# Narrow diagonal key blocks of query chunks 1 to 3 spread among the wide ones

## What is computed

```
x  = L0_attn_x                                    # 4 x 2048 x 256
xn = layernorm(x)
q, k, v = low-rank projections of xn              # rotary embedding on half of q and k
scores = (q @ k.T) / sqrt(16)                     # per batch and head, 2048 x 2048, causal
att = softmax(scores)
out = x + (att @ v) @ Wc + ffn(xn)
```

## Time and profile before

| what | value |
|---|---|
| median of 3 runs | 2284.16 us (2282.98 to 2284.55) |
| the profiled execution: its own time | 2280.11 us |
| the profiled execution: its span | 2278.3 us |
| attention: first to last product | 660.7 to 2150.2 us of the span |
| distance of one turn from the next (same instruction) | 92.75 us |
| mean granted TensorE clock | 0.943 of full |

### The profile page before, as it was taken

One profiled execution on the slowest core, in us unless ns is written; L12 is line 12 of the kernel. 1 busy time (PEld: TensorE's weight loads), 2 busy tenths in 40 slices (PEclk: granted clock), 3 DMA queues, 4 the chain that ended last, 5 costly groups with the idle time before them and its releaser, 6 DMA issues. The chain is left out here.

```text
span 2278.3 us, 50411 instructions
## 1 busy us (share of the span) xinstructions
PE 2095.3 (92%) x14033; PEld 799.9 (35%) x14033; DVE 1858.6 (82%) x4721; ACT 1560.9 (69%) x2068; POOL 338.1 (15%) x617
## 2 busy tenths in 40 slices
PE   6899999999799999999998999999999899999698
PEld 5455455455322222222222222222222222222155
DVE  5677877877789889798897988989889898899177
ACT  1655665665248778788787878878788788888600
POOL 1111111111210211102111121111211112111100
PEclk8999999999769999899998999989999999999879
DMA  3122232234330321303203032030330303300176
GB/s 148 56 76 76 83 87 61 84 86 92 93 51 2 49 36 15 50 2 48 41 10 50 2 48 41 9 50 2 48 48 2 50 2 49 48 2 12 35 225 206
DMA packets 146114, 123.95 MB, mean 54 GB/s; under 512 B 81984, under 2 KB 132500, under 8 KB 144404
## 3 DMA queue, kind: packets, MB, share of 16 engines
q1 hardware_dynamic: 137156, 112.46, 23.5%
q10 hardware_dynamic: 8720, 8.65, 1.3%
HBM read 69.50 MB, written 50.86 MB: 53 GB/s over the span
## 5 line engine op out<-in xcount | busy, mean ns | idle before, releaser
L1142 ACT ACTIVATE prob<-st 128x1024 f32<-128x1024 f32 (+3 forms) x1280 | 1080.0, 900 | 207.4 <-PE st L1265 194.3
L1241 PE MATMUL sm<-K,Q 48*128 48x512 f16 (+3 forms) x2304 | 650.8, 368 | 56.4 <-DVE pm L1204 19.4
L1204 DVE TENSOR_REDUCE pm<-sm 128x1 f32<-128x512 f32 x1024 | 648.7, 683 | 39.7 <-PE sm L1241 37.2
L1278 PE MATMUL pv<-prob,V 128*32 128x512 f32 (+3 forms) x5120 | 622.8, 562 | 0.1
L1189 DVE CUSTOM_DVE_ANT_0 sm<-sm,mask 128x128 f32<-128x128 f32 (+3 forms) x1024 | 490.6, 509 | 69.4 <-PE sm L1241 58.1
L1265 PE MATMUL st<-Q,K 50*128 50x512 f16 (+3 forms) x2560 | 496.6, 362 | 17.3 <-ACT prob L1142 14.7
L1241 PEld LDWEIGHTS sm<-K,Q 48*128 48x128 f16 x2304 | 174.3, 94 | 783.3 <-DVE pm L1189 326.8
L1094 POOL TENSOR_SCALAR_AFFINE_SELECT prob<-prob 128x256 f32<-128x256 f32 x512 | 205.7, 406 | 1284.1 <-ACT prob L1142 1279.5
L1200 DVE CUSTOM_DVE_ANT_0 sm<-sm,excess 128x512 f32<-128x512 f32 x256 | 172.9, 717 | 43.8 <-PE sm L1241 34.3
L1265 PEld LDWEIGHTS st<-Q,K 50*128 50x128 f16 x2560 | 135.0, 95 | 132.6 <-ACT prob L1142 84.9
L1278 PEld LDWEIGHTS pv<-prob,V 128*32 128x32 f32 x5120 | 104.4, 110 | 161.5 <-issue 130.3
(11 more groups left out here) (138 smaller groups left out, 1824.5 us busy)
## 6 DMA issues: line engine op xcount, KB each, us to landing
Q<-scratch_q SPq DMA_DIRECT2D x102, 128.0 KB, 4.3
K<-scratch_k SPq DMA_DIRECT2D x102, 128.0 KB, 6.5
x<-in_x SPq DMA_DIRECT2D x18, 512.0 KB, 4.6
scratch_v<-Vs SPq DMA_DIRECT2D x64, 128.0 KB, 2.0
scratch_r<-R SPq DMA_DIRECT2D x16, 512.0 KB, 3.2
V_raw<-scratch_v SPq DMA_DIRECT2D x16, 512.0 KB, 8.9
scratch_y<-Y SPq DMA_DIRECT2D x64, 128.0 KB
Yt<-scratch_y SPq DMA_DIRECT2D x16, 512.0 KB, 5.8
```

The lines of the kernel that those rows point to most:

```text
L1142: act.activation(prob[(slot * UNITS + u) % PT][:, :, 0:width], st[number % ST][:, :, 0:width], ACT.Exp)\
L1204: dve.tensor_reduce(out=pm[:, row, t, k:k + 1], in_=x, axis=AX.X, op=ALU.max).then_inc(sm_read, 1)
L1241: pe.matmul(dst[:, 0:block_width(t, k)], lhsT=Q[slot][r, h // 2, t * P:(t + 1) * P], rhs=K[slot][r, h // 2, k * CH:k * CH + block_width(t, ...
L1278: i = pe.matmul(pv[2 * DH * h:2 * DH * (h + 1), CH - width:CH], lhsT=V[slot][:, j, h, :], rhs=prob[(slot * UNITS + 2 * n + h // 2) % PT][: ...
```

## The change

The blocks of a chunk are listed by a function. Chunk 0 keeps its order. In chunks 1 to 3 the narrow blocks are set at even distances among the wide ones: chunk 1 reads 0, **5**, 1, 2, **6**, 3, 4, **7**; chunk 2 reads 0, 1, **9**, 2, 3, 4, **10**, 5, 6, 7, **11**, 8; chunk 3 reads 0, 1, 2, **13**, 3 to 6, **14**, 7 to 10, **15**, 11, 12 (narrow ones in bold). The flag that closes the accumulation and the planner's copy-out now go by the place in the list. No instruction is added or removed in the body of a turn, apart from register settings.

```diff
-ORDER = [(c, j, CH - P * max(0, j - SUB * c)) for c in range(TC) for j in range(SUB * (c + 1))]
+def key_blocks(c):
+
+
+    wide, narrow = list(range(SUB * c + 1)), list(range(SUB * c + 1, SUB * (c + 1)))
+    if c == 0:
+        return wide + narrow
+    step = len(wide) / len(narrow)
+    blocks = []
+    for n, j in enumerate(wide):
+        blocks.append(j)
+        blocks += [x for k, x in enumerate(narrow) if n < step * (k + 0.5) <= n + 1]
+    return blocks
+
+
+ORDER = [(c, j, CH - P * max(0, j - SUB * c)) for c in range(TC) for j in key_blocks(c)]
+LAST_BLOCK = [n + 1 == PAIRS or ORDER[n + 1][0] != ORDER[n][0] for n in range(PAIRS)]
...
-                if j == SUB * (c + 1) - 1:
+                if LAST_BLOCK[n]:
                     act = max(act, end + SIGNAL) + EVACUATION
...
-                                  start=j == 0, stop=j == SUB * (c + 1) - 1, tile_position=(0, 2 * DH * h))
+                                  start=j == 0, stop=LAST_BLOCK[n], tile_position=(0, 2 * DH * h))
```

## The result

| | before | changed |
|---|---|---|
| median of 4 runs | 2284.36 us | 2314.92 us |
| range | 2282.98 to 2285.65 | 2314.64 to 2316.02 |
| profiled execution, its span | 2278.3 us | 2312.7 us |
| attention, first to last copy of `pv` | 1481.1 us | 1513.6 us |
| an ordinary turn | 92.6 to 92.9 us | 94.2 to 94.5, or 95.8 to 96.2 us |

The ratio is 1.0138, 95% interval 1.0123 to 1.0153. The forecast was 2294 us, with a range up to 2312. The sign was right and the size was 31 us instead of 10. Attention holds 32.5 of the 34.4 us by which the two spans differ. The third kind of turn, the first behind each turn of the hardware loop, takes 96.5 to 97.8 us before and 98.5 to 100.3 us now.

What follows compares the result with a forecast made beforehand. TensorE was taken to pace the narrow stretches, TensorE with VectorE the wide ones. 15 turns x (1.0 - 0.4) + 1.0 for the last = +10.0 us gave 2294 us, range 2262 to 2312.

Steps and rivals of the forecast that it cites:

- Step (b): End of a turn: TensorE waits for the last wide block's mask, 0.75 to 1.25 us, booked as 1.0 us per turn.
- Step (c): End of a turn on VectorE: idle time grows from 0.56 to some 2 us, not added to Step (b).
- Step (a): Wide stretches of chunks 1 to 3: less TensorE waiting for ScalarE, 0.4 us off a turn, bounds 0 and 2.78 us.
- the term for the clock: TensorE's low clock: nothing booked in the forecast's sum; more low time appeared only as Rival 3.
- Rival 3: Turn's start: the stop lengthens TensorE's low clock, up to 1.7 us a turn, 2320 us; chance 0.08.
- Steps (d) and (e): GpSimd's `negate` and `place_v` stay hidden despite moved masks; SP's queue moves with entries and last product; nothing booked.
- Rival 1: VectorE paces: spreading closes its gaps in the narrow stretches, 1.97 us a turn, 2271 us, or 2258; chance 0.34.

Runs made afterwards that it cites:

- e3: Changed kernel, all three chunks spread, but with narrow block 15 as the last of chunk 3; ratio 1.0047 to the kernel before.
- e7: Changed kernel with a turn's last two entries moved from ahead of unit 78's scores to ahead of the last two products; ratio 1.0138 to the kernel before.
- e6: Blocks in the rising order of the kernel before, entries and excess units at the places planned for the spread order; ratio 1.0135 to the kernel before.
- e9: Against the kernel before, only chunk 3 spread, with block 15 last; ratio 0.9977.
- e8: Against the kernel before, chunks 2 and 3 spread, with block 15 last, chunk 1 in rising order; ratio 0.9996.
- e2: Against the kernel before, only chunks 1 and 2 spread, chunk 3 in rising order; ratio 1.0049.
- e12: e3 with chunk 1's last two blocks swapped, so a wide block closes it, entries planned anew; ratio 1.0010 to the kernel before.
- e4: Spread block order of the changed kernel, entries and excess units at the places planned for the rising order; ratio 1.0188 to the kernel before.
- e1: Changed kernel with only chunk 3 spread, chunks 1 and 2 in rising order; ratio 1.0056 to the kernel before.
- e10: Kernel before, in rising order, but with wide diagonal block 12 put last in chunk 3; ratio 1.0061.

## Why the prediction was wrong

**Step (b), the stop at the turn's end: right.** Said: 0.75 to 1.25 us on TensorE, ended by GpSimd's mask, 1.0 us taken, in every turn. Measured: 0.98 us, 16 times, 15.4 us. Its price by e3 is 1.15 us of chunk 3 per turn, 18 us in all against the 16 booked.

**Step (c): right in kind, too small.** VectorE's gap is 3.44 us, over the 2 to 3 us that were to show it. That it must not be added holds by e7.

**Step (a), the gain in the wide stretches: this step failed, by its sign.** With it failed the term for the clock, which the sum had at nothing (below). Step (a) said that the waits for ScalarE would shrink, that VectorE's gaps would not be touched directly by the widths, and took 0.4 us off a turn. At equal clock, turn 8 is 94.20 us against 92.61 before, or 92.65 in turns like it: +1.57 us, of which 1.15 is the turn's end, so the rest is **+0.42 us where -0.4 was booked**, 12 us over 15 turns. The waits point to why. Those for exponentials fell by 1.6 us over all of attention, a tenth of a microsecond a turn. Those of entries for a bank rose by 20.3 us, 1.3 a turn, since the planner put the entries at other places and TensorE's list is strict: an entry that is listed before VectorE has freed its bank holds up the main work behind it. That these waits are the loss is argued and not shown, since they and the time don't move in step (below), but e6 shows that new places for the entries can cost 1.35% by themselves. (Part of the 1.3 is regained: TensorE's busy time in that turn, a union of matmuls that overlap, is 87.75 against 88.27 us.) The lower bound of the step was zero gain, with no loss admitted, though the widths decide where the planner puts every entry. I read TensorE's full narrow stretches as work merely moved; they were also the stretches in which it hardly ever waited: 5.20 of 5.20, 5.09 of 5.10 and 6.19 of 6.26 us busy.

**Which chunk's spreading lost it.** Turns with equal low clock tell it: chunks 1 to 3 without any (mean of the three places of a turn in the loop), and a chunk 0 with 3.4 us of it. Before, that is 77.34 + 14.55 = 91.89 us. With chunk 3 spread (e9) it is 77.11 + 14.63 = 91.74, with chunk 2 as well (e8) 77.61 + 14.63 = 92.24, with chunk 1 as well (e3) 78.06 + 14.18 = 92.24, and with chunks 1 and 2 alone (e2) 78.32 + 14.18 = 92.50. So spreading chunk 3 did gain some 0.2 us a turn (0.15 by e9 against before, 0.26 by e3 against e2), spreading chunk 2 cost 0.5, and spreading chunk 1 cost next to nothing but the low clock at its seam, which e8 and e9 don't have. The waits for banks in e9, e8 and e3 are 32.2, 47.4 and 54.7 us: they rise with the 0.5 us of chunk 2, and again with chunk 1, where the time doesn't.

**Rival 3, the clock: the right kind at the wrong place.** It put another low spell behind the turn's start. There nothing grew: 15.1 to 15.2 us from one turn's last copy to the next, against 15.40 to 15.56 before. The new spells stand 36 us behind it, at the seam of chunks 1 and 2, in 7 turns: 7 x 1.58 = 11 us. I had named chunk 0 as the one sparse spell and did not look at what stands at a seam; turn 14 of the kernel before showed a fall at one. Its price, 1.58 us for 3.4 us of low clock, is near the 1.7 that I had.

**Steps (d) and (e): right.** Among the waits of the changed kernel's TensorE none is for `NK` or `V`, and none of its own for Q's transfers.

**Rival 1, VectorE paces: no.** No turn got shorter, and VectorE's idle time per turn rose from 92.61 - 83.03 = 9.6 to 94.20 - 82.66 = 11.5 us. But its opposite was too simple as well: VectorE is not the bound, and yet TensorE's waits for it grew by 20 us. By the Trainium skill's rule that I had weighed ("Trainium Kernel Development and Optimization", Performance Expectations), weight loads at 35% leave TensorE room. The runs show no such room at the turn's end, where the stop of 0.98 us went with 1.15 us of time (e3), and VectorE's gap was not the one to count: e7 cut its first part to 1.45 us and the time stayed as it was.

**The sum, with what was measured.** 15 turns x 1.57 = 23.6 us, low clock at the seam 11.1, the last turn 86.08 - 84.70 = 1.4: 36.1 us. Against it stand about 1 us in turn 11, whose low clock at the start was 3.4 instead of 6.8 us, 1.3 us for the low clock in turn 14 of the kernel before, and some 1.5 us in the four turns behind a loop's: 32.3, where attention shows 32.5. Of the 10 us forecast, (b) gave 16 and came to 18; (a) gave -6 and came to +6; the clock gave nothing and came to +11, less what was short elsewhere. (a) alone would have made 2306, inside the range; (a) and the clock together left it.

**Left open.** By medians the way from the changed kernel to e3 is 0.9%, to e12 another 0.37%, to e8 0.14%, to e9 0.19%; the last two are about as large as their intervals, and what spreading chunk 1 and chunk 2 cost apart rests on single executions. And in e12 the low clock is gone with the wide product at the seam and the entries planned for it, and it isn't shown which of them did it, nor why: before and e4 have a 128 wide product at the same seam and no low clock, e6 too and has it in 4 turns.

## What to carry to other kernels

When an order of main work is changed and a planner sets side work by it, the side work's new places are part of the change. Count the waits of the strictly ordered engine by what ends them, before and after: here exponentials 14.7 to 13.1, banks 34.8 to 55.1, masks 0 to 15.4 us, and only the first was what spreading was about. In this case such a count named the places to look at, but not the price: 20 us more of waits for banks stood beside some 6 us of loss. Close a loop body with the item whose dependent chain (exponential, mask) is shortest, since in a strict list nothing of the next turn stands beside it: worth 18 us of 31 here. Try a spreading one chunk at a time: chunk 3's gained 0.2 us a turn, chunk 2's lost 0.5. And compare turns of equal low clock.

## What the hardware showed

- TensorE's clock fell to its lower level behind 4.5 us in which it was busy for 4.13, not only behind a sparse spell: 3.4 us at 0.52, 1.58 us lost. It did so in 7 of 15 full turns, with the same instructions in all of them.
- The time at the lower level came as 3.4 or 6.8 us in ordinary turns, in e6 also as some 10 us. In e9 the same place, behind the start of such a turn, has either, with 14.6 and 15.1 to 15.6 us for the stretch: up to 1 us a turn by nothing in the code. A turn that is compared must have the same low time.
- The first copy of `pv` came at 669.5 to 674.4 us of the span in the kernel before, e1, e6, e8, e9 and e10, whose TensorE has the same instructions up to there. So 5 us of a single span can't be given to an edit; medians over several runs and distances inside attention can.
